# Small loads and constants later, the gate ahead of a copy, the mask matmuls ahead of a product

## What is computed

```python
# layer 0: 6 heads of 64, scores masked by adj
q, k, v = x @ Wq + bq, x @ Wk + bk, x @ Wv + bv
probs = softmax(q @ k.T / 8 + where(adj, 0, NEG))
x = layernorm(x + (probs @ v) @ Wf + bf)
# layer 1: 12 heads of 32
h = x @ W;  th = tanh(h)
attn = leaky_relu(th @ w_src + (th @ w_dst).T, 0.2)
attn = softmax(where(adj, attn, -999))
f = elu(attn @ h + b)
gate = sigmoid(x @ H_w.T + H_b)
out = layernorm(x + gate * f + (1 - gate) * x)
```

## Time and profile before

| | |
|---|---|
| median of three runs | 1215.51 us |
| the profiled execution | 1212.56 us, of which the span from first to last instruction is 1210.8 us |
| mean granted TensorE clock | 0.985 |
| busy: PE / PEld / DVE / ACT / POOL | 1119.5 / 897.3 / 1029.2 / 885.1 / 550.1 us |
| instructions | 25654 |

### The profile page before, as it was taken

How to read it: one execution, slowest core, us unless ns; L and a number is a source line. 1 busy time by engine, 2 the same in 40 slices (tenths; PEclk the granted TensorE clock), 3 DMA queues, 4 the chain that set the end, 5 groups by cost and what they waited for, 6 DMA issues and landing times.

```text
span 1210.8 us, 25654 instructions
## 1 busy us (share of the span) xinstructions
PE 1119.5 (92%) x8364; PEld 897.3 (74%) x8428; DVE 1029.2 (85%) x2086; ACT 885.1 (73%) x3319; POOL 550.1 (45%) x717
## 2 busy tenths in 40 slices
PE   0989999999999999999999999999999999998874
PEld 0767787788778777887878778777877877786652
DVE  2527989989898998989899898989899898988886
ACT  2236878788778878877887787778787877877775
POOL 3324445445443635553454445444445454444332
PEclk9989999999999999999999999999999999998997
DMA  6401001010010101010010101002010100100000
GB/s 161 138 6 32 30 14 67 14 60 15 18 63 7 67 15 60 15 45 36 8 66 15 67 8 67 15 8 66 14 67 15 60 15 8 41 14 15 15 14 20
DMA packets 25894, 44.67 MB, mean 37 GB/s; under 512 B 2462, under 2 KB 23714, under 8 KB 25762
## 3 DMA queue, kind: packets, MB, share of 16 engines
q1 hardware_dynamic: 22368, 41.29, 9.9%
q10 hardware_dynamic: 3362, 1.73, 0.8%
q0 software_dynamic: 32, 0.00, 0.0%
HBM read 30.43 MB, written 12.58 MB: 36 GB/s over the span
## 4 chain that ended last, share of the span: by engine, by line
ACT 36%; PE 33%; DVE 16%; issue 8%; POOL 4%; ACTq 2%; POOLq 0%; DVEq 0%
ACT z L581 20%; PE ps_b L247 9%; PE ps_a L247 8%; PE ps_d L247 5%; ACT p L608 5%; DVE z L910 5%; POOL xT_lo L923 3%; PE ps_d L450 3%; ACT p1T L591 2%; DVE s L773 2%; PE ps_s L350 2%; ACT gate L657 2%; DVE p1T L757 2%; ACT ctxT_hi L646 2%; DVE s L892 2%
## 5 line engine op out<-in xcount | busy, mean ns | idle before, releaser
L581 ACT ACTIVATE z<-z,s 128x128 f32<-128x128 f32 x768 | 298.9, 403 | 0.5 <-DVE s L798 0.5
L945 POOL TENSOR_SCALAR s<-s 128x1 f32<-128x1 f32 x128 | 28.6, 224 | 339.7 <-DVE s L894 311.6
L608 ACT ACTIVATE p<-ps_s,s 128x128 f32<-128x128 f32 x384 | 135.4, 372 | 57.9 <-DVE s L773 57.8
L960 POOL TENSOR_TENSOR p<-p,s 128x768 f32<-128x768 f32 x64 | 94.2, 1472 | 147.7 <-DVE s L804 147.7
L581 ACT ACTIVATION_READ_ACCUMULATOR z<-z,s 128x1 f32 x768 | 155.5, 202 | 0.0
L450 PE MATMUL ps_d<-ident,z 128*128 128x128 f32 x768 | 120.9, 281 | 18.1 <-ACT z L581 9.1
L674 ACT ACTIVATE z<-ps_d 128x512 f32<-128x512 f32 x192 | 100.4, 595 | 42.7 <-remote 42.7
L968 POOL TENSOR_TENSOR thw<-th,w_sd 128x768 f32<-128x768 f32 x64 | 117.8, 1840 | 5.2 <-ACT th L629 5.1
L910 DVE SCALAR_TENSOR_TENSOR z<-ps_d,z 128x512 f32<-128x512 f32 x192 | 118.7, 674 | 0.0
L450 PEld LDWEIGHTS ps_d<-ident,z 128*128 128x128 f32 x768 | 91.2, 142 | 33.5 <-ACT gate L657 17.6
L599 ACT ACTIVATE x1T_hi<-ps_b 128x384 fp32r<-128x384 f32 x64 | 31.5, 492 | 100.5 <-PE ps_b L397 100.5
(11 more groups left out here) (158 smaller groups left out, 3521.3 us busy)
## 6 DMA issues: line engine op xcount, KB each, us to landing
x_cols<-in_xT_dram SPq DMA_DIRECT2D x16, 768.0 KB, 6.5
xb<-in_x_dram SPq DMA_DIRECT2D x16, 768.0 KB, 4.9
out_dram<-y SPq DMA_DIRECT2D x64, 192.0 KB, 1.8
z<-in_L_gnn_Wq_dram SPq DMA_DIRECT2D x1, 576.0 KB, 6.7
p1T<-in_L_gnn_Wk_dram SPq DMA_DIRECT2D x1, 576.0 KB, 9.0
qT<-in_L_gnn_Wv_dram SPq DMA_DIRECT2D x1, 576.0 KB, 11.5
kT<-in_L_gnn_Wf_dram SPq DMA_DIRECT2D x1, 576.0 KB, 13.8
z<-in_L_gnn_W_dram SPq DMA_DIRECT2D x1, 576.0 KB, 4.0
```

Of the source, the lines that this page charges most:

```text
L581: done = act.activation(z[:, a, :], z[:, a, :], ACT.Exp, bias=neg1[:, a:a + 1], accum_out=sum1[:, a:a + 1])
L608: last = act.activation(p0[:, o, i, :], ps_s[:, o, i * N:(i + 1) * N], ACT.Exp, bias=neg0[:, k:k + 1], accum_out=sum0[:, k:k + 1])
L960: pool.tensor_tensor(p0[:].rearrange("p o i n -> p (o i) n"), p0[:].rearrange("p o i n -> p (o i) n"), inv0.unsqueeze(2).broadcast_to([P, ...
```

## The change

Small loads: the seven move from ScalarE's queue to SP's, behind the fourth weight and ahead of W1 and Hw. Constants: VectorE makes them at the end of the first group and not in its step 0; the bias product, the addition of bf and the two additions to xb move behind the value products. GpSimd makes one quarter of the mask at the start and the other three in the first three steps of g = 1, where it also moves H_b's parts and adds 1 to b1. The gate is made ahead of the second copy to p1T. The scores' two mask matmuls become a function of their own, `scores_mask`, that runs at the end of the step before, ahead of `apply_p1`.

```diff
@@ sync
             for n, name in enumerate(W_ORDER):
+                if n == 4:
+                    sp.dma_start(bv_col[:], bv).then_inc(S["const_in"], 16)
+                    sp.dma_start(choose[:], pick_in).then_inc(S["const_in"], 16)
+                    for s, w in enumerate((w_src, w_dst)):
+                        sp.dma_start(w_sd[:, s, :], w.partition_broadcast(P)).then_inc(S["const_in"], 16)
+                    sp.dma_start(bf_in, bf.partition_broadcast(P)).then_inc(S["const_in"], 16)
+                    sp.dma_start(b1_all[:], b1.partition_broadcast(P)).then_inc(S["const_in"], 16)
+                    sp.dma_start(hb_row, Hb.rearrange("(o d) -> o d", o=1)).then_inc(S["const_in"], 16)
                 if n >= 4:
                     sp.wait_ge(S["weight_lo"], n - 3)
@@ tensor
+            def scores_mask(t):
+
                 if due(t):
                     pe.wait_ge(S["p0T_even"], t)
-                if due(t):
                     pe.wait_ge(S["p0T_odd"], t)
+                if t % (B // 4) == 0:
+                    pe.wait_ge(S["mask_ready"], t // (B // 4) + 1)
+                if t == 0:
+                    pe.wait_ge(S["consts_ready"], 3)
+                    pe.wait_ge(S["bf_ready"], 1)
+                for o in range(2):
+                    pe.matmul(ps_s[:, o, 0:C * N].rearrange("p (i n) -> p i n", i=C), ident_53[:],
+                              mask[:, t, :].unsqueeze(1).broadcast_to([P, C, N]), start=True, stop=False)
+
+            def scores(g, par, j):
...
                     if att:
-                        if n == 1 and j == 0:
-                            pe.wait_ge(S["consts_ready"], 3)
-                            pe.wait_ge(S["mask_ready"], 4)
-                            pe.wait_ge(S["bf_ready"], 1)
-                        scores(ta, g, 1 - par, j)
+                        if ta == 0:
+                            scores_mask(0)
+                        scores(g, 1 - par, j)
...
-                    if n == 0 and j == 3:
-                        bias_product()
...
                     if qkv:
                         fill_b(g, n, j)
+                    if n == 0 and j == 3:
+                        bias_product()
...
                     if gat:
                         logits(tl)
+                    if 0 <= ta and ta + 1 < B:
+                        scores_mask(ta + 1)
                     if tail:
                         apply_p1(tl - 1, (j + 1) % 2, gat)
@@ scalar
             act.dma_start(adj_u8, adj_dram).then_inc(S["adj_in"], 16)
-            act.dma_start(bv_col[:], bv).then_inc(S["const_in"], 16)
-            act.dma_start(choose[:], pick_in).then_inc(S["const_in"], 16)
...
                     if tail:
                         exp1(tl - 1, 8, 12)
-                    if tail:
-                        turned_p1(tl - 1, 1)
                     if gat:
...
                         act.activation(gate[:, tl % 3, :], ps_d[:, 2, 0:D], ACT.Tanh,
                                        scale=0.5).then_inc(S["gate_ready"], 1)
+                    if tail:
+                        turned_p1(tl - 1, 1)
@@ vector
-                    if n == 0 and j == 0:
-                        small_constants()
...
                     if n == 0 and j < 3:
                         weight_parts(3 + j)
+                    if n == 0 and j == 3:
+                        small_constants()
+                        dve.wait_ge(S["bvf_made"], 1)
+                        dve.tensor_tensor(bf_all[:], ps_s[:, 0, 0:D], bf_in, ALU.add).then_inc(S["bf_ready"], 1)
@@ gpsimd
+            mask_quarter(0)
...
+                    if n == 0 and j == 3:
+                        xb_with_bias(g, par, slice(0, 2))
+                        xb_with_bias(g, par, slice(2, 4))
...
+                    if n == 1 and j == 0:
+                        moved_constants()
+                    if n == 1 and j < 3:
+                        mask_quarter(j + 1)
```

45 lines of the change are left out of this document (17 added, 28 removed).

## The result

The changed kernel takes 1195.12 us (median of four runs, 1193.95 to 1199.2) against 1215.1 us for the kernel before on the same chip: a ratio of 0.985, 95% interval 0.982 to 0.988. The forecast was 1194.0, range 1186 to 1203. The span of the profiled execution went from 1210.8 to 1192.0, 18.8 us less.

What follows compares the result with a forecast made beforehand. The start was held by ScalarE's queue, stalled 14.13 us at bv_col's issue; the steady part waited for the gate at one place. Start -16.3 and steady part -5.0 gave -21.3 from 1215.51: 1194.0 us, range 1186 to 1203.

Steps and rivals of the forecast that it cites:

- Part 1: Start: seven small loads leave ScalarE's queue for SP's, so TensorE starts at 11.4 and not 29.73: -18.3 us.
- Part 2: End of prologue: constants and bias product move behind the value products, delaying the scores' mask matmuls: +1.2 us.
- Part 3: First step: TensorE's wait for xT_lo now runs beside the bias product and the constants: -2.2 us.
- Part 4: First group: GpSimd's moved work (hb DMA, b1 addition, mask quarter) delays its second scaling: +3.0 us; next two steps 0.
- Part 5: Steady part: gate ahead of the second p1T copy gains 0.12 us in 42 of 56 steps: -5.0 us, bounds 0 and -9.0.
- Part 6: Steady part: mask matmuls ahead of the second layer's product; fT later but within its slack: 0.
- SP held: Rival: SP's queue is held at bv_col instead, so W1 comes late: +2.5 us, 1196.5; chance 0.15.
- POOL pays each step: Rival: GpSimd's moved mask quarters also cost 2.2 us in each of the next two steps: 1198.4; chance 0.08.
- steady part gives all of it: Rival: moving the gate gains the full 0.16 us in each step, -9.0 us: 1190.2; chance 0.07.
- stall stays: Rival: something else holds ScalarE's first work, so nothing starts earlier and only the gate's gain remains: 1210 to 1215; chance 0.04.
- fT late: Rival: fT comes too late for TensorE's transposes, 0.50 us in 62 steps: +14.7 us, 1230.2; chance 0.04.

Runs made afterwards that it cites:

- the copy: The changed kernel run again unaltered, as the measure for the runs beside it: 1195.59 us, ratio 0.987.
- constants in idle time: Changed kernel with VectorE's scaled identities behind the third split weight and its other small constants behind the second graph's copy of v: 1191.19 us, ratio 0.983.
- loads only: Kernel before the change with only the seven small loads moved to SP's queue, ahead of W1: 1207.01 us, ratio 0.996.
- mask quarter early: Changed kernel with the mask's second quarter made right behind the first on GpSimd: 1195.11 us, ratio 0.986.
- matrix late: Kernel of constants in idle time, with ScalarE issuing the adjacency matrix and making bq8 only behind its third weight: 1192.93 us, ratio 0.985.
- gate back: Changed kernel with the gate again behind the second copy to p1T: 1196.72 us, ratio 0.987.
- masks back: Changed kernel with the next scores' mask matmuls again behind the second layer's product: 1196.66 us, ratio 0.987.
- start only: Changed kernel with both steady-part moves (gate and mask matmuls) undone, only the start's parts left: 1197.37 us, ratio 0.988.
- matrix on SP: Kernel before the change with the adjacency matrix issued by SP behind its fourth weight, small loads staying on ScalarE: 1199.51 us, ratio 0.990.
- constants spread: Kernel of matrix late, with the small constants in three pieces behind the fourth, fifth and sixth split weights: 1191.15 us, ratio 0.983.

## Why the prediction was right, and where it was not

**Part 1, -18.3:** right, -18.7 measured, by the mechanism named, and the runs make it sharper: it is not the number of loads on ScalarE but that they stood behind the matrix. The 1.34 and 0.9 us taken for VectorE's parts without GpSimd beside them came out as 1.35 and 0.92. That W1 costs nothing held too, but by luck: it landed 11.5 us after its issue at 10.91 and not 4.0, at 22.4, and VectorE came to it only at 22.89 and not at 20.8. In the copy VectorE waited 0.30 us for it.

**Part 2, +1.2:** mis-sized. From the first matmul to the first mask matmul it is 4.8 us more. From the end of the value products to the first mask matmul it is 7.57 us (32.38 to 39.95) where the term had 4.8. The term took 3.71 us for the constants; they took 6.29 (33.05 to 39.34), because two of them ran beside GpSimd's xT_lo. The text had used this very effect in part 1 (3.81 for a pair against 0.9 for one) and did not ask in part 2 what GpSimd does at the new place. Another 0.8 us are slower products ahead of that. The timeline of the change shows matmuls 0.43 us apart and then 0.23:

```profile
15.87 0.63 PE L255 MATMUL ps_b<-xT_lo,wq_hi 128*128 128x512 f32 x1
16.29 0.63 PE L255 MATMUL ps_b<-xT_hi,wq_hi 128*128 128x512 f32 x1
...
17.23 0.40 PE L255 MATMUL ps_b<-xT_hi,wq_hi 128*128 128x512 f32 x1
17.46 0.40 PE L255 MATMUL ps_b<-xT_hi,wq_lo 128*128 128x512 f32 x1
```

The second product takes 2.9 us (15.01 to 17.92); before, it took 2.05 (33.54 to 35.59).

**Part 3, -2.2:** right in kind, too large. The wait of 2.19 us for xT_lo is gone, but the step from graph 0 to 1 with the clock at 1.00 takes 12.01 us in the new order (*constants in idle time*, 38.19 to 50.20) and 13.24 in the old (*loads only*, 50.79 to 64.03): -1.2.

**Part 4, +3.0:** right in place, half the size: 1.55, by *mask quarter early*. The quarter takes 1.91 us and the addition to b1 0.32, where 2.2 and 1.40 were taken from rows in which VectorE ran beside them. The DMA issue and the addition cost nothing: *mask quarter early* keeps them at this place, and its step takes 11.98 us, *loads only*, without them, 11.97. The next two steps cost nothing, as forecast (15.14 and 15.13 us for the first of them).

**The clock** is a term that the prediction did not have. The same three steps took 44.94 us before, where the granted clock fell to 0.79 and 0.87 in two of them, and 40.34 in *loads only*, which has the same code there and 1.00 throughout; in the change 42.09, with 0.79 in the first, and 40.69 in *matrix late*, which has the change's order in these steps and 1.00 throughout. So the falls in these steps cost 4.6 us in the one profile and 1.4 in the other. Another fall lies ahead of them: in the change 1.82 us pass from the first mask matmul to the first maxima, with a granted clock of 0.70 from 40.00 on, where the kernel before has 1.41 us: 0.4 more. The start's -16.4 is then: -18.7 + 0.8 + 4.0 - 1.2 + 1.55 = -13.6 from the code and -4.6 + 1.4 + 0.4 = -2.8 from the clock. That the forecast of -16.3 met the number is luck: part 2 cost 3.6 us more than forecast and part 3 gave 1.0 less, while part 1 gave 0.4 more, part 4 cost 1.4 less, and the clock, which was no term, gave 2.8. What decides when the clock falls stays open. One pattern stands in the rows: in the six profiles in which TensorE waits 3.54 us for `bf_all` (the change, its copy, *gate back*, *masks back*, *start only*, *mask quarter early*), 1.8 to 2.4 us pass from the first mask matmul to the first maxima; in the eight others it is 1.40 to 1.42.

**Part 5, -5.0:** the mechanism is right, the term too large: -2.9 to -3.1. The term stood between 0 and 0.16 per step, and its "middle", 0.12, is not the middle of these bounds; 0.08 in 42 steps would have been 3.4. The copy followed `cols_R` by 0.08 before, and follows it by 0.04 in the rows of the change beside *gate back*. So it is 0.05 in each of the 57 steps. The fourth step of each group, which the prediction left out, gains it too (0.05 on average, before against after), although the wait for xT_lo grew from 4.5 to 9.5 us, as this row of the list of waits of the changed kernel, 101 to 1079 us, says (total, times, longest):

```profile
PEld ps_a L255 <- POOL xT_lo L929: 9.5, 14, 0.7
```

**Part 6, 0:** right (0.5 us for 57 steps, within the spread).

**The rivals.** *SP held*: not in the change (the longest of the seven issues took 2.07 us, the longest of all on SP in its first 16 us 2.91), but a real effect: it is what happens with the matrix on SP. *POOL pays each step*, *steady part gives all of it*, *stall stays*, *fT late*: none happened. In the sum, terms of -18.3, +1.2, -2.2, +3.0, -5.0 and 0 were -18.7, +4.8, -1.2, +1.55, -2.9 and 0, with -2.8 by the clock and +0.4 at the end: 18.8 us of span, 21.3 forecast. (1215.51 less 21.3 is 1194.2, not 1194.0.)

Two kernels of the study beat the change in the median by 4 us, *constants in idle time* and *constants spread*; their intervals overlap that of the change (0.982 to 0.988).

## What to carry to other kernels

When an engine stands at the issue of a small load, look at what the load before it in that queue is: moving the slow one to the end of its queue was one line here and gave as much as the whole change, and 11 us more than moving the seven loads alone (1196.1 against 1207.0). When work moves to another place in VectorE's or GpSimd's order, read at the new place what the other of the two does there, since a cast of 0.35 us took 2.04 here. And read a wait's worth from the gap that is left on the engine behind it (0.05 us), not from its length (0.29).

## What the runs showed of the hardware

- A load behind the adjacency matrix in the same queue holds the issuing engine until about 17 to 21 us: 14.13 us on ScalarE, 8.30 on SP. The issues behind the held one took 0.45 to 0.90 us again. While the matrix was under way but no issue was held, the other queue's issues took 0.33 to 2.91 us.
- A VectorE cast of one partition takes 0.35 us alone and 1.94 to 2.04 beside GpSimd's conversion of the mask; a cast and a scaling of 128 x 128 took 1.17 and 1.84 beside its subtraction, 0.21 alone.
- TensorE's granted clock fell for several us in the first three steps in 12 of 14 profiles, not at the same place in all, and cost up to 4.6 us; it did not in *loads only* and *matrix late*. The same kernel's graph 3 came at 83.86 and 82.88.
- The first matmuls of the execution start 0.43 us apart up to 33.28 before the change (3.6 us) and up to 16.72 after it (5.7 us), and 0.23 behind that. The profile gives a granted clock of 1.00 for both stretches. In a later stretch of the change, 42.25 to 43.96, the spacing is 0.43 too, and there the granted clock is 0.50 (42.25 to 43.90).
